# A vision tower on one core: feed-forward with transposing transfers, landmark reading with zero products, and another order in the global attention

## The reference

```python
# landmarks read the tokens of their block (H=32 heads, DH=16, M=4 landmarks, S=64 tokens)
ra = softmax(einsum('bhnmd,bhnsd->bhnms', l2q, kb) * scale)
ro = einsum('bhnms,bhnsd->bhnmd', ra, vb)
# tokens read all landmarks (global attention)
ga = masked_softmax(einsum('bhqd,bhkd->bhqk', q, gk) * scale, g_mask)
out_global = einsum('bhqk,bhkd->bhqd', ga, gv)
out = (1.0 - gate) * out_local + gate * out_global
h = h + out @ w_out + b_out
# feed-forward on layernorm(h), width 2048, q = block quantization
gate = q_act(x) @ q_w(w_gate).T ; up = q_act(x) @ q_w(w_up).T
inter = silu(gate) * up
h = h + q_act(inter) @ q_w(w_down).T
```

## Time and profile before

| | |
|---|---|
| median of 3 runs | 1832.39 us (1829.31 to 1834.97) |
| profiled execution | 1829.61 us |
| its span, first to last instruction | 1827.8 us |
| PE busy | 1548.6 us, 85% of the span |
| DVE busy | 1327.4 us, 73% |
| ACT busy | 1040.8 us, 57% |
| POOL busy | 539.7 us, 30% |
| mean granted TensorE clock | 0.867 of full speed |

### The profile page before, as it was taken

The page is one execution under the profiler, slowest core; times in us unless marked ns, Lnnn a source line. Parts: engine busy times, 40 slices in busy tenths (PEclk is TensorE's granted clock), DMA queues, the critical chain, the costliest instruction groups (busy, mean ns, idle before and its releaser), DMA issues. The chain is left out here.

```text
span 1827.8 us, 35108 instructions
## 1 busy us (share of the span) xinstructions
PE 1548.6 (85%) x11908; PEld 1069.0 (58%) x12006; DVE 1327.4 (73%) x2446; ACT 1040.8 (57%) x2579; POOL 539.7 (30%) x583
## 2 busy tenths in 40 slices
PE   2177749999999999999677896598988499999998
PEld 2177626676676677667456685465656244444543
DVE  8999746777777777777324362388887489999997
ACT  7799527887888887887412241366665233333332
POOL 0000014544544554444200000044444233333332
PEclk8555569999999999999786656799998799999999
DMA  2022252222223222222220363344454101111111
GB/s 58 2 61 61 61 172 86 75 75 99 87 75 106 85 75 99 75 87 90 76 85 0 127 207 110 117 148 148 151 157 129 46 29 46 46 46 46 46 46 52
DMA packets 122044, 154.77 MB, mean 85 GB/s; under 512 B 52480, under 2 KB 54144, under 8 KB 121984
## 3 DMA queue, kind: packets, MB, share of 16 engines
q1 hardware_dynamic: 121984, 154.01, 26.1%
HBM read 94.21 MB, written 59.77 MB: 84 GB/s over the span
## 5 line engine op out<-in xcount | busy, mean ns | idle before, releaser
L1057 PE MATMUL al_ps<-al_w,al_xT 128*128 128x512 f32 (+2 forms) x1024 | 350.9, 496 | 0.0
L1057 PEld LDWEIGHTS al_ps<-al_w,al_xT 128*128 128x128 f32 x1024 | 191.8, 192 | 127.0 <-issue 107.5
L2125 ACT ACTIVATE ff_zT<-ff_psz 128x1024 bf16<-128x1024 bf16 x64 | 65.5, 1024 | 239.4 <-PE ff_psz L2216 239.4
L2144 POOL TENSOR_TENSOR ff_zq<-ff_z,ff_back 128x1024 bf16<-128x1024 fp8e4 x64 | 122.2, 1909 | 252.0 <-DVE ff_z L2173 252.0
L442 PE MATMUL tk_ps<-tk_w,tk_l 128*128 128x64 f32 x512 | 113.0, 422 | 79.5 <-DVE tk_w L411 52.4
L442 PEld LDWEIGHTS tk_ps<-tk_w,tk_l 128*128 128x128 f32 x512 | 110.4, 332 | 82.1 <-issue 82.1
L739 POOL TENSOR_TENSOR al_qv<-al_qv,al_qe 128x512 f32<-128x512 f32 x48 | 62.0, 1291 | 248.2 <-PE al_ps L1130 248.2
L2224 PE MATMUL ff_acc<-wdT,ff_zT 128*128 128x512 bf16 x512 | 123.0, 384 | 2.2 <-ACT ff_zT L2125 2.2
L2199 PE MATMUL ff_gate<-wgT,xqT 128*128 128x512 bf16 x496 | 121.5, 383 | 3.8 <-ACTq L107 3.0
L2199 PE MATMUL ff_up<-wuT,xqT 128*128 128x512 bf16 x481 | 120.6, 383 | 1.6
L993 DVE TENSOR_REDUCE al_mx<-al_ps 128x32 f32<-128x2048 f32 x32 | 73.3, 2292 | 58.1 <-PE al_ps L1130 58.1
(11 more groups left out here) (308 smaller groups left out, 3520.0 us busy)
## 6 DMA issues: line engine op xcount, KB each, us to landing
al_hx<-h_s SPq DMA_DIRECT2D x36, 256.0 KB, 2.8
o_s<-al_o SPq DMA_DIRECT2D x32, 272.0 KB, 2.1
h_s<-tk_w SPq DMA_DIRECT2D x16, 512.0 KB, 3.8
v_s<-al_v SPq DMA_DIRECT2D x32, 256.0 KB, 2.1
k_s<-al_kT SPq DMA_DIRECT2D x32, 256.0 KB, 2.4
q_s<-al_qT SPq DMA_DIRECT2D x32, 256.0 KB, 2.6
lt_kT<-k_s SPq DMA_DIRECT2D x16, 512.0 KB, 4.6
lt_v<-v_s SPq DMA_DIRECT2D x16, 512.0 KB, 3.7
```

Of the source, the lines that this page charges most:

```text
L1057: ins = pe.matmul(out, xT[:, T, k], w[:, k, cols], start=False, stop=True, skip_group_check=True)
L2144: pool.tensor_tensor(zq[:, u].rearrange("p (k s) -> p k s", s=QB), z8[:, u].rearrange("p (k s) -> p k s", s=QB), back[:, u, :, None].to_br ...
```

## The change

Three stages are edited.

In `landmarks_from_tokens` a tile `still` of zeros (512 columns, bf16) is set by POOL, and PE multiplies it with the identity into a PSUM bank that nobody reads: eight such products before the first scores, and in each element two after the transposes and two after the scores.

In `attention_global` the order within a turn differs on two engines. DVE: `exponents` moves behind the first half of the residual, `quantized` behind the statistics. ACT: `normalised` moves behind `exp`. Two products that only set the state of PSUM banks read `wdT` in place of the mask.

In `ffn` the eight transposes on PE and ACT's copy go; SP issues a transposing transfer from `ff_zq` to `ff_zT` in their place. `down` of a unit comes one unit later on PE. The residual is written into the accumulator by ACT before the products, which then all add to it, and ACT copies the result out, so that DVE's L2158 goes. The loops are written out.

```diff
@@ landmarks_from_tokens
+            pool.memset(still[:], 0.0).then_inc(s_still, 1)
             pool.memset(pT[:], 0.0).then_inc(s_zero, 1)
...
+            def stream():
+                for _ in range(2):
+                    pe.matmul(ps[:, 6], K.identb[:], still[:], start=True, stop=True)
+
+            pe.wait_ge(s_still, 1)
+            for _ in range(4):
+                stream()
             scores(0)
             for i in range(BATCH):
                 transposes(i)
+                stream()
                 if i + 1 < BATCH:
                     scores(i + 1)
+                stream()
                 sums(i)
@@ attention_global, ACT
-                if some(j):
-                    normalised(j)
                 if some(j - 1):
                     quantized(j - 1)
                 if some(j + 3):
                     exp(j + 3)
+                if some(j):
+                    normalised(j)
@@ attention_global, DVE
                 if some(j + 1):
                     gated(j + 1)
-                if some(j - 1):
-                    exponents(j - 1)
                 if some(j + 2):
                     sums(j + 2)
                 if some(j):
                     residual(j, 0)
                 if some(j - 1):
-                    quantized(j - 1)
+                    exponents(j - 1)
                 if some(j):
                     residual(j, 1)
                     statistics(j)
+                if some(j - 1):
+                    quantized(j - 1)
@@ ffn, SP
+            def turn(i, j):
+                q, u = i * NU + j, j % 2
+                sp.wait_ge(zq_r.sem, zq_r.upto(q))
+                sp.wait_ge(dn_p.sem, dn_p.done(q, 2))
+                sp.dma_start_transpose(zT[:, u], zq[:, u]).then_inc(zt_in[u].sem, 16)
...
+            for i in range(BATCH):
+                turn(i, 0)
+                if i:
+                    store(i - 1, 1)
+                turn(i, 1)
+                if i + 1 < BATCH:
+                    residual(i * 2 + 2, 0)
+                turn(i, 2)
+                if i + 1 < BATCH:
+                    residual(i * 2 + 3, 1)
+                turn(i, 3)
+                store(i, 0)
@@ ffn, ACT
-                    act.activation(zT[:, u], psz[:, u], ACT.Copy).then_inc(zt_r.sem, 1)
...
+            def residual(i, T):
+                act.wait_ge(h1_in[T].sem, h1_in[T].upto(i))
+                act.wait_ge(y_r.sem, y_r.done(i * 2 + T, 2))
+                act.activation(acc[:, T], h1[:, T], ACT.Copy).then_inc(res_r.sem, 1)
...
+            for i in range(BATCH):
                 for j in range(NU):
+                    silu(i, j)
+                    if i and j in (0, 2):
+                        result(i - 1, j // 2)
+                        residual(i, j // 2)
@@ ffn, DVE
-                dve.tensor_tensor(y[:, T], acc[:, T], h1[:, T], ALU.add).then_inc(y_r.sem, 1)
@@ ffn, PE
-            def transposes(q, u):
...
                     if ahead:
                         gates(q + 2, t2, hf2)
-                    transposes(q, u)
-                    if ahead:
                         ups(q + 2, t2, hf2)
-                    down(q, i * 2 + j // 2, j // 2, j % 2, u)
+                    if j:
+                        down(i, j - 1)
+                    elif not first:
+                        down(i - 1, NU - 1)
```

More of the change, by code:

```diff
@@ L1383, in landmarks_from_tokens @@
         s_k, s_v = [[sem(f"{n}_in{u}") for u in range(2)] for n in ("k", "v")]
-        s_zero, s_ql, s_sc, s_max, s_exp, s_rec, s_norm, s_tr, s_copy, s_sum, s_lmx, s_pick = (sem(n) for n in (
-            "zero", "ql", "sc", "max", "exp", "rec", "norm", "tr", "copy", "sums", "lmxr", "pick"))
+        s_zero, s_ql, s_sc, s_max, s_exp, s_rec, s_norm, s_tr, s_copy, s_sum, s_lmx, s_pick, s_still = (sem(n) for n in (
+            "zero", "ql", "sc", "max", "exp", "rec", "norm", "tr", "copy", "sums", "lmxr", "pick", "still"))
         block = ctx.enter_context(nc.Block())
@@ L1968, in _ @@
         def _(pe):
+            for bank in op_bank:
+                ins = pe.matmul(ps[:, bank], K.identb[:], K.wdT[:, 0], start=True, stop=True)
+            ins.then_inc(s_bits, 1)
             pe.wait_ge(s_set, 2)
[L1970 to L1973 removed]
             def project(i, T):
@@ L2111, in _, with silu @@
         def _(act):
-            sg_r.credit(act)
-            zt_r.credit(act)
-            def silu(q, u):
+            for q in (sg_r, y_r, res_r):
+                q.credit(act)
+            act.wait_ge(s_bits, 1)
+            def silu(i, j):
+                q, u = i * NU + j, j % 2
                 act.wait_ge(g_p.sem, g_p.upto(q))
@@ L2137, in _ @@
             zq_r.credit(pool)
-            with pool.Fori(0, BATCH) as i:
+            for i in range(BATCH):
                 for j in range(NU):
@@ L2179, in element @@
                     unit(i, j, ls)
-                    if j == 1 and not first:
-                        result(i * 2 - 1, i - 1, 1)
-                    if j == 3:
-                        result(i * 2, i, 0)
                 ls.end()
-            element(0, True)
-            with dve.Fori(1, BATCH) as i:
-                element(i, False)
-            result(BATCH * 2 - 1, BATCH - 1, 1)
+            for i in range(BATCH):
+                element(i)
         @block.tensor
         def _(pe):
-            for q in (g_p, up_p, zt_p, dn_p):
+            for q in (g_p, up_p, dn_p):
                 q.credit(pe)
+            for T in range(2):
+                ins = pe.matmul(acc[:, T], K.identb[:], K.wdT[:, 0], start=True, stop=True)
+            ins.then_inc(s_bits, 1)
             def project(bank, wT, done, t, hf):
@@ L2210, in ups, with down, element @@
                 project(up, K.wuT, up_p, t, hf)
-            def transposes(q, u):
-                pe.wait_ge(zq_r.sem, zq_r.upto(q))
-                pe.wait_ge(zt_r.sem, zt_r.done(q, 2))
-                for k in range(2 * KC):
-                    ins = pe.transpose(psz[:, u, k], zq[:, u, k * P:(k + 1) * P], K.identb[:])
-                ins.then_inc(zt_p.sem, 1)
-            def down(q, t, T, hf, u):
-                pe.wait_ge(zt_r.sem, zt_r.upto(q))
+            def down(i, j):
+                q, u, T, hf = i * NU + j, j % 2, j // 2, j % 2
+                pe.wait_ge(zt_in[u].sem, zt_in[u].upto(i * 2 + T))
                 if hf == 0:
-                    pe.wait_ge(y_r.sem, y_r.done(t, 2))
+                    pe.wait_ge(res_r.sem, res_r.upto(i * 2 + T))
                 for k in range(2 * KC):
                     ins = pe.matmul(acc[:, T], zT[:, u, k], K.wdT[:, 2 * KC * hf + k],
-                                    start=(hf == 0 and k == 0), stop=(hf == 1 and k == 2 * KC - 1))
+                                    start=False, stop=True, skip_group_check=True)
                 ins.then_inc(dn_p.sem, 1)
-            def element(i, more):
+            def element(i, first=False, last=False):
                 for j in range(NU):
-                    q, u = i * NU + j, j % 2
-                    ahead = more or j < NU - 2
+                    q = i * NU + j
+                    ahead = not last or j < NU - 2
                     t2, hf2 = i * 2 + (j + 2) // 2, j % 2
@@ L2242, in _ @@
                 ups(q, 0, q)
-            with pe.Fori(0, BATCH - 1) as i:
-                element(i, True)
-            element(BATCH - 1, False)
+            element(0, first=True)
+            for i in range(1, BATCH - 1):
+                element(i)
+            element(BATCH - 1, last=True)
+            down(BATCH - 1, NU - 1)
 class Kept:
```

67 lines of the change are left out of this document (29 added, 38 removed).

## The result

| | before | after |
|---|---|---|
| median of 4 runs beside each other | 1832.28 us | 1783.42 us (1778.12 to 1791.20) |
| ratio, 95% interval | | 0.9737 (0.9694 to 0.9780) |
| profiled execution | 1829.61 us | 1778.12 us |
| its span | 1827.8 us | 1776.3 us |
| PE / DVE / ACT / POOL busy, us | 1549 / 1327 / 1041 / 540 | 1509 / 1307 / 1022 / 561 |

The change made the kernel 49 us faster. A second set of 6 runs of the same kernel gave 1781.93 us and 0.9742 (0.9715 to 0.9768). The prediction was 1773 with a range of 1756 to 1815: the direction was right for the whole and for each of the three parts, and the time came out 10 us above the forecast.

What follows compares the result with a forecast made beforehand. Bounds: PE in the feed-forward, a ring of engines in global attention, PE at half clock in landmarks. - 23 - 21 - 14 = - 58 us from 1829.6 gave 1771.6; with the median 2.8 above, 1773 us, range 1756 to 1815.

Steps and rivals of the forecast that it cites:

- Forecast - 23: Feed-forward total: - 26 us from the units, + 2.2 at the stage's end, + 0.7 at its start.
- DVE as bound by a hair: Feed-forward: DVE at about 5.23 us a unit becomes the bound over PE's 5.19, instead of 5.64: 26 us less.
- The latency was taken as 4: Feed-forward: the transposing transfer's landing, between 2.7 and 11.5 us, taken as 4; nothing waits up to 6.
- The tail, + 2.2 in the forecast: Feed-forward's end: the transfer's latency is exposed once, where 1.8 us passed before, adding 2.2 us.
- The rival of a slow transfer: Feed-forward: transposing transfer too long for two buffers, 6.75 us a unit at 11.5 us latency; 1876 us, chance 0.10.
- the prediction's other estimate: Feed-forward: at 261 GB/s for transposing transfers, 256 KB would stream in 1.0 us; not used in the sum.
- Forecast - 21: Global attention total: DVE's wait for ACT goes, a turn falls from 15.9 to 14.4 us, 1.5 us over 14 turns.
- slack (a): Global attention: POOL's `scaled`, about 1.9 us, is covered only by the second half with statistics, 2.22: 0.2 us of slack.
- (b): Global attention: PE's transposes of `ag_xq` and `sums` wait for DVE's rounding; 2.55 us against softmax's 2.66, 0.1 slack.
- the sum of pieces, 14.2: Global attention: DVE's pieces of a turn, start to start, add up to 14.2 us; the rest of 15.9 is waiting.
- Forecast - 14: Landmarks total: zero products bring full clock, a turn falls from 5.15 to 4.4 us (- 11), and 3 at the end.
- 238 GB/s, "fitting": Landmarks: DMA must bring 1 MB in a 4.4 us turn, where it brought 196 GB/s; fitting, without much room.

Runs made afterwards that it cites:

- e10: Changed kernel with DVE's scaling by the inverse in each feed-forward unit done on half of the columns: 1776.95 us, ratio 0.9713 to the kernel before.
- e14: The changed kernel itself again, with more rounds: 1781.93 us, ratio 0.9742 to the kernel before.
- e3: Kernel before with only the new order in global attention taken over: 1812.66 us, ratio 0.9907.
- e5: Changed kernel with POOL's gated sum in global attention made of one half of the tile only: 1777.21 us, ratio 0.9720 to the kernel before.
- e7: Changed kernel with PE's transposes of the quantised tile in global attention one place later, behind the next turn's projection: 1777.08 us, ratio 0.9722 to the kernel before.
- e8: Changed kernel with 18 zero products, not 8, at the landmark stage's start and 12 more behind the first scores: 1780.73 us, ratio 0.9746 to the kernel before.
- e12: Changed kernel with the next element's keys ahead of the values on SP's queue in the landmark stage: 1776.80 us, ratio 0.9726 to the kernel before.
- e9b: Changed kernel with each transposing transfer of the feed-forward done twice, one after the other: 1797.84 us, ratio 0.9835 to the kernel before.
- e2: Kernel before with only the landmark part of the change taken over: 1818.05 us, ratio 0.9936.
- e6: Changed kernel with DVE's two reductions ahead of the maximum with the floor, beside POOL's gated sum: 1773.66 us, ratio 0.9690 to the kernel before.
- e13: Changed kernel with four edits: DVE's reductions together, later transposes on PE, more zero products, keys ahead of values: 1762.71 us, ratio 0.9646 to the kernel before.

## Why the prediction was right, and where its sizes were off

**Feed-forward: right to 3 us.** Forecast - 23, measured - 26.1, and 353.0 us or - 24.4 in the second profiled run. The unit came out at 5.22 where 5.23 was read off one start of before, with DVE as bound by a hair and PE at 5.18 (e10). The start costs 0.4 us where 0.7 was taken. The latency was taken as 4 and is 3.1. The tail, + 2.2 in the forecast, is - 0.2 (16.3 us from the last product's start to the end before, 16.1 after), and that it is below nothing is luck of the clock. After, the last eight products ran at full clock:

```profile
1765.72 1.91 POOL L2184 TENSOR_TENSOR ff_zq<-ff_z,ff_back 128x1024 bf16<-128x1024 fp8e4 x1 [3.31 <-DVE ff_z L2207]
...
1770.75 1.90 PE L2249 MATMUL ff_acc<-wdT,ff_zT 128*128 128x512 bf16 x8 [1.79 <-DMA ff_zT<-ff_zq]
```

1770.75 - 1767.63 = 3.1 us, 1.3 more than before, against 3.25 - 1.90 = 1.35 less for the products. In the second run of the same kernel (e14) they took 3.39 us and the tail 17.6:

```profile
1776.10 3.39 PE L2249 MATMUL ff_acc<-wdT,ff_zT 128*128 128x512 bf16 x8 [3.30 <-DMA ff_zT<-ff_zq]
```

With the feed-forward of before it goes both ways as well: 3.25 us in the profiled run of before, 1.90 in e3, where the tail is 15.0. At like clock the tail grew by 1.1 to 1.3 us, which is the term as the prediction built it, with a latency of 3.1 in place of 4. Of the nine profiled runs with this feed-forward two have a tail of 16.1 us (after and e5) and seven one of 17.4 to 17.8.

The rival of a slow transfer fell: 3.1 us for eight blocks of 128x128, where the estimate from the Trainium skill's figure (VectorE: DVE Perf Modes, The three transpose paths) was 10.5 us. That figure is for one block, and eight in one transfer are not eight times that. How much of the 3.1 us is streaming, which the prediction's other estimate put at 1.0, no run tells.

**Global attention: right in kind, 5 us too much.** Forecast - 21, measured - 15.5. The wait for ACT went as forecast, from 15 times and 29.3 us to once and 5.0 us. Neither slack (a) nor (b) turned into a wait of the steady turn ((b) once, 1.3 us, in a turn of 15.9); TensorE's own wait for the rounded tile, about 1.3 us a turn, costs nothing. Two steps were off, by about the same. The turn of before is 15.7 us and not 15.9: the sum over the earlier trace rows held more than 15 turns, while the two starts of L1607 in the earlier trace rows, 1317.65 and 1333.33, lie 15.68 apart. That alone is 0.17 x 14 = 2.4 us of the 21. The other step is the sum of pieces, 14.2, "no instruction is added, only moved". It is 14.59 in the middle, 0.19 over the forecast's 14.4, 2.7 us in 14 turns. The piece "sums 2.78" was read where L1889 took 0.73 us, itself held by POOL's other product beside it, and in the new order it stands beside `gated_sum` and takes 1.33. The piece grew by 0.60 us, and the second half with statistics shrank by 0.18, which makes 14.6 of 14.2. The row of before, by tile, showed the range all along (the median is not the free value):

```profile
L1889 DVE TENSOR_TENSOR ag_sm<-ag_sm,ag_floor x16: 225/732/1620, 1169.9 to 1401.4; 128x64 f32<-128x64 f32 x16
```

```profile
L1900 DVE TENSOR_TENSOR ag_sm<-ag_sm,ag_floor x16: 225/1332/1803, 1160.5 to 1372.6; 128x64 f32<-128x64 f32 x16
```

Turns longer than 14.59 occur as longer ones than 15.73 did before; what is new in the drain is PE's waits, 3 us (e7).

**Landmarks: right in kind, 3 us too much.** Forecast - 14, measured - 10.9. The 3 us at the stage's end came as forecast (3.0); the turns gave 7.9 and not 11. The clock came to 1.00 and a turn at that clock takes 4.23, better than the 4.4 taken, since the scores halved as well (0.65 us):

```profile
1057.96 0.17 DVE L1458 RECIPROCAL lt_sum<-lt_sum 128x4 f32<-128x4 f32 x1
1058.64 0.44 PE L1512 MATMUL lt_ps<-cst,lt_pa 128*128 128x128 f32 x2 [0.51 <-DVE lt_pa L1460]
1059.44 0.65 PE L1501 MATMUL lt_ps<-lt_kT,lt_ql 128*32 128x64 f32 x32
...
1062.19 0.17 DVE L1458 RECIPROCAL lt_sum<-lt_sum 128x4 f32<-128x4 f32 x1
```

The mean of 4.62 has two causes that the sum left out, both shown: idle times ahead of the first turns, in which the clock fell (e8: 3.6 us), and late keys, which the faster turn made late (e12). The prediction weighed the rate of the transfers (238 GB/s, "fitting") and not when they may start.

## What to carry to other kernels

Before moving instructions, look at the spread of each one's duration: where the maximum is far over the minimum at one shape, compare its end with the ends on the other engines. If they coincide it is a hold, and it moves with the order. Put DVE's reductions or its reads from PSUM beside a long POOL instruction, and its other SBUF-only operations elsewhere. And count a turn between two starts of the same step: an instruction that comes twice a turn gives too long a one. Where TensorE's clock is the gain, price every idle time ahead of its products twice: once for itself, once for what it may do to the clock of the products behind it; and when a loop becomes faster, look first at where on its queue the next load stands.

## What the runs showed of the hardware

- **A DVE instruction waits for the end of POOL's.** The 64-column maximum took 0.22 us alone and up to 1.8 beside POOL, and ended 0.08 to 0.12 us behind POOL's instruction. A 32-column tensor_scalar on integers did much the same in the kernel before (1.99 us at 1269.20, ending at 1271.18, POOL's sum at 1271.14). Reductions, and instructions with one operand in PSUM, were not held. The Trainium skill states this (SBUF — State Buffer, Who interferes with whom): the two engines share a port pair as an exclusive lock, which a VectorE instruction with two SBUF inputs or in a two-port mode takes, and a reduction does not. The traces agree in each case named here; whether the tensor_scalar ran in a two-port mode they do not show. It works the other way too: POOL's 2-column product L1771 took 1.18 us beside DVE's product into `ag_xq` and 0.20 elsewhere, once a turn after; before, where this product of DVE stood elsewhere, none of POOL's tiny steps was over 0.4 us.
- **One transposing transfer of 128x1024 in bf16 landed in 3.1 us**, 256 KB from SBUF to SBUF, at any time of the stage, also when two followed each other (e9b, 3.0 to 4.9), beside plain transfers.
- **TensorE's clock fell behind some small waits and not behind others of the same length.** In the landmark stage with zero products it went to half behind waits for keys of 0.86 us (e5), 0.95 (e8), 0.98 (e2) and 1.29 (e6). It stayed at full behind 0.94 us (after, 1073.15), 1.04 (e7), 1.06 and 1.21 (e8), 1.11 (e14) and 1.23 (e9b). In e5, e6 and e8 another wait for keys, of 0.93, 0.63 and 1.06 us, came some 10 us before the one that the clock fell behind; in after a wait of 0.52 us came as close behind one of 0.94 and left it at full. The 0.51 us that PE waits in every turn for the normalised weights left it at 1.00 throughout. That late keys bring the fall is shown: in e12 and e13, whose keys never come late behind the first scores, no later turn is slow. What makes the difference between two equal waits was not tried.
